# Two transformer-like blocks over 16 batches on one core: attention products regrouped between large products, and a new order of work on all engines

## What is computed

```python
x = x + 0.5 * ffn0(layernorm(x))      # 128x128 weights rounded to int4, plus bias and a rank-16 term
x = x + attn0(layernorm(x))           # 8 heads of 16: (Q K^T * decay, causal) V, group norm, silu gate, W_O
x = x + 0.5 * ffn0(layernorm(x))
x = x + 0.5 * mod(layernorm(x))       # every token: x + w * mlp(x) for the half of the tokens chosen by score
x = x + attn1(layernorm(x))           # 4 heads, key 32, value 64: chunk retention, rms norm, gate, Wo
x = x + 0.5 * mod(layernorm(x))

def mod(h):
    scores = h @ w_router             # top k = 256 of 512 tokens in each batch
    top_scores, top_idx = top_k(scores, 256)
    processed = gelu(h[top_idx] @ W1 + b1) @ W2 + b2
    return h.at[top_idx].add(sigmoid(top_scores) * processed)
```

## Time and profile before

| | |
|---|---|
| median of 3 executions | 839.02 us |
| profiled execution, its span | 841.55 us, 839.7 us |
| TensorE busy | 748.2 us (89%), 12963 matmul records |
| VectorE, GpSimd, ScalarE busy | 681.2 us (81%), 442.1 us (53%), 420.2 us (50%) |
| granted TensorE clock, mean | 0.969 of full speed (2.4 GHz) |
| the chain that ended last | TensorE 60%, VectorE 29%, GpSimd 4%, issue 3%, ScalarE 3%, DMA 1% |

### The profile page before, as it was taken

The page is one execution under the profiler, slowest core; times in us unless marked ns, Lnnn a source line. Parts: engine busy times, 40 slices in busy tenths (PEclk is TensorE's granted clock), DMA queues, the critical chain, the costliest instruction groups (busy, mean ns, idle before and its releaser), DMA issues.

```text
span 839.7 us, 29454 instructions
## 1 busy us (share of the span) xinstructions
PE 748.2 (89%) x12963; PEld 613.5 (73%) x12963; DVE 681.2 (81%) x1832; ACT 420.2 (50%) x838; POOL 442.1 (53%) x363
## 2 busy tenths in 40 slices
PE   4887999999999889978799999999999999999750
PEld 3766888888787777866677887878787888777530
DVE  4789999989899999885758898887777888886667
ACT  1345556556555545553355545556556545555321
POOL 3368888888887777876332443344342334343210
PEclk9999999999999999999999999999999999999885
DMA  6000000000000000010000000000000000000213
GB/s 220 28 28 28 28 28 27 28 28 27 28 27 9 22 28 2 3 53 1 2 2 2 3 3 3 2 2 2 2 3 2 3 2 2 2 2 2 63 38 100
DMA packets 23138, 18.56 MB, mean 22 GB/s; under 512 B 2001, under 2 KB 20322, under 8 KB 22754
## 3 DMA queue, kind: packets, MB, share of 16 engines
q1 hardware_dynamic: 22306, 16.13, 6.2%
q10 hardware_dynamic: 704, 0.54, 0.2%
HBM read 12.48 MB, written 4.19 MB: 20 GB/s over the span
## 4 chain that ended last, share of the span: by engine, by line
PE 60%; DVE 29%; POOL 4%; issue 3%; ACT 3%; DMA 1%; DVEq 0%; SPq 0%
PE ps L263 13%; PE ps L373 11%; PE ps L382 7%; PE ps L258 4%; PE ps L599 3%; PE ps L274 3%; DVE sc L1113 2%; DVE t L1461 2%; DVE x L1085 2%; PE ps L284 2%; PE ps L356 2%; DVE t L1146 2%; PE ps L591 2%; PE ps L336 2%; ACT h L729 2%
## 5 line engine op out<-in xcount | busy, mean ns | idle before, releaser
L948 POOL TENSOR_TENSOR grstd<-gve,mhalf 128x32 f32<-128x32 f32 (+1 forms) x32 | 133.7, 4179 | 88.7 <-DVE gve L1140 88.3
L373 PE MATMUL ps<-xt_r,w_s 128*128 128x512 f32 x256 | 131.2, 626 | 6.6 <-DVE gate L1370 4.7
L382 PEld LDWEIGHTS ps<-w_s,hid 128*128 128x128 f32 x1024 | 122.4, 194 | 2.2 <-issue 0.8
L382 PE MATMUL ps<-w_s,hid 128*128 128x128 f32 x1024 | 123.8, 277 | 0.1
L719 ACT ACTIVATE hid<-ps,b_s 128x512 f32<-128x512 f32 x128 | 88.1, 704 | 47.3 <-PE ps L373 46.0
L944 POOL TENSOR_TENSOR r_ret<-ve_ret,powers 128x8 f32<-128x8 f32 x32 | 58.0, 1813 | 53.2 <-DVE ve_ret L1071 53.2
L939 POOL TENSOR_TENSOR rstd_ln_mod<-ve_ln_mod,mhalf 128x4 f32<-128x4 f32 x32 | 32.3, 1010 | 90.6 <-DVE ve_ln_mod L1071 90.6
L1113 DVE TENSOR_TENSOR sc<-ps,tri 128x1024 f32<-128x1024 f32 (+1 forms) x64 | 59.4, 953 | 24.8 <-PE ps L295 13.4
L263 PEld LDWEIGHTS ps<-w_qkvg,xt_p 128*128 128x128 f32 x512 | 64.4, 198 | 12.2 <-issue 6.9
L263 PE MATMUL ps<-w_qkvg,xt_p 128*128 128x128 f32 x512 | 68.8, 284 | 3.7 <-ACT xt_p L715 2.7
L373 PEld LDWEIGHTS ps<-xt_r,w_s 128*128 128x128 f32 x256 | 43.2, 198 | 36.1 <-ACT hid L719 8.1
(11 more groups left out here) (196 smaller groups left out, 1719.5 us busy)
## 6 DMA issues: line engine op xcount, KB each, us to landing
out_x<-base SPq DMA_DIRECT2D x16, 256.0 KB, 2.4
xin<-in_x SPq DMA_DIRECT2D x15, 256.0 KB, 2.9
xtin<-in_xt SPq DMA_DIRECT2D x15, 256.0 KB, 3.2
rot<-in_rot SPq DMA_DIRECT2D x2, 1024.0 KB, 7.7
w_s<-in_w SPq DMA_DIRECT2D x2, 256.0 KB
xin<-in_x ACTq DMA_DIRECT2D x1, 256.0 KB, 7.0
w_qkvg<-in_wqkvg SPq DMA_DIRECT2D x1, 256.0 KB, 7.8
xtin<-in_xt ACTq DMA_DIRECT2D x1, 256.0 KB, 8.0
```

The lines of the kernel that those rows point to most:

```text
L373: nc.tensor.matmul(bank(k), w1_s[:, f, :], xt["r"][:].rearrange("p j n -> p (j n)"), start=True, stop=True).then_inc(s[f"h{f}"], 1)
L382: mm = nc.tensor.matmul(bank(k, j * P, P), hid[:, f, j * P:(j + 1) * P], w2_s[:, f, :], start=False, stop=(f == last and j == NT - 1), ski ...
L948: nc.gpsimd.tensor_tensor(grstd[:, 0:n], gve[:, 0:n], mhalf[:, 0:n], ALU.pow) \
```

## The change

It changes four things.

1. **Small products in smaller groups, between large ones.** `scores`, `states`, `carry_a` take the chunks that they do as an argument. In slot A attend goes in four groups of one chunk, carry stands between the two halves of the query and key product, and states goes in two groups of two chunks around the transposes of queries and keys. In slot B scores and states go in two groups of two chunks, and the two parts of carry are parted by the query and key product.
2. **A new order on all engines and new PSUM banks.** In slot A the routed down products of a batch start the slot, each between others, the large products are permuted, and so are ScalarE's, GpSimd's and VectorE's lists. In slot B all down products stand before the states, which now end the slot.
3. **The last choice's sums** (`rank_sum(3, f, 5)`) stand between the last down products, and its score transposes (`rank_rows`) one product earlier.
4. Waits are moved with them; no arithmetic is added or removed.

The diff, cut to its core:

```diff
+AT = {"score": 1, "ffn1": 7, "xt_p": 0, "qk": 6, "v": 5, "g": 1, "tg": 0, "wo": 0, "xt_c": 7, "ffn2": 7,
+      "xt_r": 1, "mod": 5, "tqk": 0, "state": 6, "up": (6, 2, 0, 5), "rank": (3, 2)}
...
-            def states_a(sl):
-                for c in range(NT):
+            def states_a(chunks, last, sl):
+                for c in chunks:
...
             def slot_a(sl, route, finish):
+                if finish:
+                    routed_down(0, AT["mod"], last, 0, 2)
...
+                    if sl.score:
+                        wait(pe, "um", now)
                     tilewise(tiles(AT["ffn1"]), xtin[sl.buf(1)][:].rearrange("p (j n) -> p j n", j=NT), w_ffn[:],
                              "ffn1")
...
+                if finish:
+                    routed_down(1, AT["mod"], last, 0, 2)
...
+                    wait(pe, "qm", now)
+                    scores_a((2, 3), 2)
+                    scores_a((0, 1), 2)
+                if finish:
+                    routed_down(3, AT["mod"], last, 0, 2)
...
+                    wait(pe, "gate", new)
+                    if route:
+                        wait(pe, "act2", done)
                     transpose_qk(AT["tqk"], new)
+                if sl.score:
                     if route:
                         wait(pe, "act1", done)
...
+                if sl.prepare:
+                    states_a((0, 1), True, sl)
...
             def slot_b(sl):
-                scores_b()
-                wait(pe, "x1", new)
+                scores_b((2, 3), 2)
                 transpose4("ln_ret", x1[sl.buf(1, 4)], BT["xt_p"])
+                scores_b((0, 1), 2)
...
                 carry_b(0, sl)
                 wait(pe, "ln_ret_xt", new)
                 tilewise(tiles(BT["qk"]), xt["p"], w_qkv1[:, 0:P])
                 tilewise(tiles(BT["qk"] + 1), xt["p"], w_qkv1[:, P:2 * P], "qk")
+                carry_b(1, sl)
...
+                wait(pe, "yn", now)
+                states_b((2, 3), False, BT["state"], sl)
                 transpose_qk(BT["tqk"], new)
+                states_b((0, 1), True, BT["state"], sl)
...
                 for f in range(NF):
                     routed_down(f, 2, now)
+                    rank_sum(3, f, 5)
 
             run_slots(slot_a, slot_ab, slot_b, slot_end)
-            for r in range(ROUNDS):
-                rank_sum(3, r, X1)
+            for r in range(NF, ROUNDS):
+                rank_sum(3, r, 5)
...
             def slot_b(sl):
                 now, new, old = sl.count(0), sl.count(1), sl.count(-1)
                 g = sl.g
-                causal(1, HC, sl)
-                causal(0, HC, sl)
...
+                if g in ROUND:
+                    rank_narrow(ROUND[g][0], ROUND[g][1] + 1, BT["rank"][1])
                 if sl.ahead:
                     block_statistics(sl.batch(2))
+                keep_states_b(BT["state"], new)
+                keep_base(sl.batch(-1), old)
```

More of the change, by code:

```diff
@@ L282, in scores_a, with scores_b @@
                             rows = slice(32 * g, 32 * g + 32)
[L283 to L284 removed]
+                            at = PS[keys, (AT["score"] + g) * BANK + c * P:(AT["score"] + g) * BANK + (c + 1) * P] \
+                                .rearrange("p (e n) -> p e n", e=2)
+                            mm = nc.tensor.matmul(at, qkt[rows, 1, tokens], qm[rows, :, tokens], start=(c == first),
                                                   stop=True, skip_group_check=True)
[L286 to L289 removed]
+                if c != first and c != first + 1:
+                    mm.then_inc(s["sc"], 1)
+            def scores_b(chunks, first):
+                for c in chunks:
                     for e in range(2):
@@ L295, in scores_b @@
                             mm = nc.tensor.matmul(PS[keys, at:at + HC],
-                                                  qkt[rows, 1, tokens], qkt[rows, 0, tokens], start=(c == 0),
+                                                  qkt[rows, 1, tokens], qkt[rows, 0, tokens], start=(c == first),
                                                   stop=True, skip_group_check=True)
-                mm.then_inc(s["sc"], 1)
-            def states_a(sl):
-                for c in range(NT):
+                if c != first and c != first + 1:
+                    mm.then_inc(s["sc"], 1)
+            def states_a(chunks, last, sl):
+                for c in chunks:
                     for e in range(2):
@@ L309, in states_a, with states_b @@
                                                   start=True, stop=True, skip_group_check=True)
-                mm.then_inc(s["state"], 1)
-            def states_b(k, sl):
-                for c in range(NT):
+                if last:
+                    mm.then_inc(s["state"], 1)
+            def states_b(chunks, last, k, sl):
+                for c in chunks:
                     for e in range(2):
@@ L320, in states_b, with carry_a @@
                                                   skip_group_check=True)
-                mm.then_inc(s["state"], 1)
-            def carry_a(sl):
-                for i in range(1, NH):
+                if last:
+                    mm.then_inc(s["state"], 1)
+            def carry_a(halves):
+                for i in halves:
                     c, e = i // 2, i % 2
@@ L1346, in slot_a @@
                     rank_choose()
+                if route:
+                    keep_base(sl.batch(-2), done)
+                if g == 0:
+                    prepare_rest()
+                if g == 1:
+                    prepare_bias()
+                if sl.prepare:
+                    products(AT["qk"], new)
                 if sl.complete:
@@ L1494, in _ @@
                 rank_try(r)
[L1495 removed]
+                rank_narrow(3, r, 5)
             rank_above()
```

414 lines of the change are left out of this document (193 added, 221 removed).

## The result

The changed kernel took 833.17 us, median of 7 executions (830.59 to 836.47); the kernel before took 839.32 us beside it, also 7 (838.67 to 841.24). The ratio is 0.9923 with a 95% interval of 0.9901 to 0.9945, so it is **6.2 us faster**, more than the 1.7 us that the prediction called the bound. 834.6 us were predicted, inside 827.5 to 843.5. The profiled execution took 834.6 us with a span of 832.8 us, 6.9 less than before. The time is right; not all of the parts that make it up are.

The account below looks back on a forecast made before the run. TensorE's own time was taken to count in 22 slots, VectorE's in five. Terms +0.9 - 2.0 - 0.8 + 0 - 2.5 = -4.4 us gave 834.6 us by the median, range 827.5 to 843.5.

Parts of the forecast that it names:

- Borders and fresh groups in slot A: TensorE in slot A: more group borders cost +1.03 us, faster group starts save 0.42, so +0.61 us a slot.
- Instruction stops: TensorE's "issue" waits in attend: all 8.0 us go in the less dense order, about half (-4.0 us) in plain slots.
- The plain slots' term: Eight plain slots of phase A: 4.9 us more TensorE work less 4.0 us of stops, +0.9 us (-3 to +5).
- VectorE's five slots: Five phase A slots with the choice, paced by VectorE: stops gone and steadier filling give -2.0 us (-5 to 0).
- First slots and the mixed slot: First slots and mixed slot: one us of stops goes, scores wait for the masked queries instead of x1; -0.8 us (-2 to +2).
- Slot B: 14 slots of phase B: TensorE work +3.5 us, half the idle time -3.5 us, together 0 us (-4 to +6).
- Tail: Kernel end: the last choice's first sum runs at 811.0 instead of 813.54, the chain moves whole; -2.5 us (-4.3 to -1.7).
- The masked queries: Rival: masked queries reach TensorE's scores late in 14 or so slots; 0.5 us late is +7 us, 841.6 us; chance 0.2.
- Groups start fast: Denies the rival that fresh small groups run at the steady pace, losing 3.4 us in A, 4.5 in B: 842.5 us; chance 0.08.
- the stops did not stay: Denies the rival that instruction blocks come late in attend whatever the density: 4 + 1 us back, 839.6 us; chance 0.15.
- More goes: Rival: all phase B idle time goes (-3.6 us more) and 3 us more in VectorE's slots: 828.0 us; chance 0.17.

Follow-up runs that it names:

- e2: The changed kernel with slot A's four attend chunks joined again behind the second part of the query and key product: 839.04 us, ratio 1.000 to the kernel before.
- e11: The changed kernel with slot B's scores in one group and its states in one group: 828.12 us, ratio 0.9859 to the kernel before.
- e1: The kernel before with only the tail's part of the change, all slots as before: 836.85 us, ratio 0.997 to the kernel before.
- e8: The kernel before with VectorE's negative mean moved behind the second causal mask in slot A: 835.45 us, ratio 0.9955 to the kernel before.
- e3: The changed kernel with GpSimd's router product back ahead of the retention norm's power in slot A: 832.53 us, ratio 0.9935 to the kernel before.

## Why the prediction was right

The time came out within 1.4 us, and so close a hit is luck: two errors nearly cancelled, some +5 us in the first slots with the mixed part and -7 us in the choice slots. Step by step:

- *Borders and fresh groups in slot A* (+0.61 us a slot). A slot without a stop took 21.72 us before and takes 22.40 now: **+0.68**. Groups run as forecast, 0.38, 0.28 and 0.59 us. Right.
- *Instruction stops* (-8.0, half of it in plain slots). From 8.0 to 0.3 us, and 3.6 us of the 8.0 had stood in plain slots. Right; that density is the cause rests on e2 alone. The plain slots' term of +0.9 measured +2.3 us: 0.9 of the difference is slot 2 (23.74 us; before 22.82), where the new waits of the first slots reach in, at a granted clock of 0.87.
- *VectorE's five slots* (-2.0, bounds -5 to 0). **Measured -9.1: the failed step.** I took VectorE's work as given ("the same VectorE work stands in another order") and looked for gains in its 8.7 us of idle time only. Its work was not given: 8.3 us in four slots were holds, in plain sight as instructions of 1.1 us on four numbers. The Trainium skill has the rule (SBUF — State Buffer, SBUF: two separate sides): VectorE with two SBUF inputs and a GpSimd instruction that reads SBUF share one pair of ports, and whoever begins second is blocked for the whole instruction. The trace agrees for GpSimd's products. It doesn't for its powers: in slot 10 the variance's first line (`mv_ln_mod`) took 0.17 us from 274.29, inside a power (`grstd`) that ran from 268.53 for 6.34 us.
- *First slots and the mixed slot* (-0.8, bounds -2 to +2). **Measured +4.2 (+5.5 and -1.3), outside the bounds.** I weighed only the scores' wait. The failed reason is the one sentence that cost banks and moved waits at nothing because "they are covered by the products between": in slots 0 and 1 there are no routed products, and in slot 2 the first up product comes only at 84.6 us, so nothing covers them. TensorE's idle time up to slot 2 grew from 20.0 to 25.1 us: a wait of the scores for x1 went (3.6 us), and waits for the copied states (2.9 us), x3 (2.4), the rotated keys (2.2) and y (1.4) stand open instead.
- *Slot B* (TensorE +3.5, idle -3.5, together 0). TensorE's work grew by 3.9 us (320.99 to 324.93), idle time fell by 5.5 (7.06 to 1.58): -1.5. Right in kind; the idle share was under-sized. The second part of carry saved less than I took: its two parts need 0.61 and 0.78 us, where one group needed 1.53, so 0.14 us and not 0.30. e11 shows that two of its six groups gave nothing: without them another 2.5 us go.
- *Tail* (-2.5). Measured -2.8, and 2.5 by e1. Right.
- *Rivals.* The masked queries cost 0.1 us in a plain slot, not 0.5: the room was just enough, as gelu no longer stands between the copies. Groups start fast, the stops did not stay. "More goes" was half right: B kept 1.6 of 7.1 us idle, and VectorE's slots gave 7 us beyond the forecast, not the 3 named.

## What to carry to other kernels

Ask of the bound engine not only where it idles but whether its instructions last what they should: group them by shape and look for one that takes several times as long as its like, then see which GpSimd product runs beside it; moving a single VectorE instruction gave 3.8 us (e8). Look for this where VectorE sets the pace: the same hold cost nothing in slots that TensorE bounds (e3). Cost an order of work separately for the stretches that lack its usual cover, above all the first slots, and keep the old order there if it is better. Here splitting attend cost 0.06 us a group and gave other engines time (e2), while in slot B, where TensorE never waited, joining the groups was faster (e11).

## What the runs showed of the hardware

- A GpSimd product of two SBUF tensors (128x512, 1.28 us) holds a VectorE instruction that starts behind it and has two inputs in SBUF, until it ends: up to 1.23 us instead of 0.15 to 0.17, by how early it begins. The hold moves to whatever such instruction comes next (e3, e8). VectorE products with one input in PSUM beside it kept their 1.22 us (`ra` in e8, `rb` 16 times before), and so did the statistics, which have one input (0.28 us each).
- The new order has holds of its own in phase B: in 8 of its slots one sum of two SBUF inputs (`x<-yall,wcol,base`, 128x128) takes 1.37 instead of 0.34 us beside the router product, and six comparisons of the choice take 0.55 instead of 0.15 us beside the sums of the states. TensorE sets the pace there (324.93 of 326.51 us).
- If VectorE begins first, GpSimd is the one that waits: the router product took 1.43 instead of 1.28 us where the product with the gate had begun 0.4 us before it (e8).
- The first 32 records of a small group start about 8 ns apart in attend and in slot B's states (0.24 us for 31 of them), 5 ns in slot A's states, 14 ns in slot A's scores. In slot B groups need the same split or joined: two groups of scores 0.42 us each, one of twice the size 0.84. What a border costs there lies in the large product beside it, 0.1 us on either side.
